# Attention and mixture of experts on one core: interleaved masked tiles, a product with ones for the last sort, and a leaner start

## The reference

```python
# layer 1: causal attention with rotary positions, then a layernorm
Q, K, V = x @ wq.T, x @ wk.T, x @ wv.T        # 16 heads of 8
Q, K = apply_rope(Q), apply_rope(K)
scores = where(causal, Q @ K.T / sqrt(8), -inf)
x = layernorm(x + softmax(scores) @ V @ wo.T)
# layer 2: plain attention over the layernormed rows, no mask
y = x + msa(layernorm(x, ln1_w, ln1_b), w_qkv, w_proj)
# experts: the row's best expert by argmax of the gate
z = layernorm(y, ln2_w, ln2_b)
e = argmax(z @ gate_w + gate_b)               # first one wins a tie
y = y + gelu(z @ w1[e]) @ w2[e]               # 128 -> 512 -> 128
out = layernorm(x + y)
```

## Time and profile before

| | |
|---|---|
| median of 3 runs | 896.61 us (893.73 to 900.15) |
| profiled execution | 894.7 us, span 893.0 us |
| PE, PEld | 809.2 us (91%), 369.5 us (41%) |
| ACT | 775.7 us (87%) |
| DVE | 328.5 us (37%) |
| POOL | 228.5 us (26%) |
| chain that ended last | PE 76%, DVE 8%, ACT 4%, issue 4%, DMA 2% |
| DMA | 51.60 MB, mean 58 GB/s |

### The profile page before, as it was taken

One profiled execution on the slowest core, in us unless ns is written; L12 is line 12 of the kernel. 1 busy time (PEld: TensorE's weight loads), 2 busy tenths in 40 slices (PEclk: granted clock), 3 DMA queues, 4 the chain that ended last, 5 costly groups with the idle time before them and its releaser, 6 DMA issues.

```text
span 893.0 us, 24266 instructions
## 1 busy us (share of the span) xinstructions
PE 809.2 (91%) x9940; PEld 369.5 (41%) x9952; DVE 328.5 (37%) x948; ACT 775.7 (87%) x906; POOL 228.5 (26%) x367
## 2 busy tenths in 40 slices
PE   8689999999999998999999999999999999996271
PEld 4244444444443443444344444444444444443240
DVE  5434525312430014320042433255332363334763
ACT  3579889999999998999999999999999899994440
POOL 5542211111110010000003343323334141443382
PEclk9799999999999999999999999999999999998575
DMA  8977220202110431810201000301000010001001
GB/s 273 269 210 224 96 49 2 95 2 49 49 48 1 108 84 40 244 50 3 48 2 32 1 3 3 78 8 37 3 3 19 14 43 3 1 3 31 30 14 41
DMA packets 34644, 51.60 MB, mean 58 GB/s; under 512 B 4064, under 2 KB 15072, under 8 KB 34528
## 3 DMA queue, kind: packets, MB, share of 16 engines
q1 hardware_dynamic: 32992, 46.30, 18.2%
q0 software_dynamic: 1536, 3.67, 1.3%
HBM read 29.12 MB, written 20.84 MB: 56 GB/s over the span
## 4 chain that ended last, share of the span: by engine, by line
PE 76%; DVE 8%; ACT 4%; issue 4%; DMA 2%; SPq 2%; POOL 2%; POOLq 1%; another core or an unknown queue 1%; DVEq 0%; ACTq 0%
PE ps L488 72%; ACT probs L922 3%; PE ps L493 3%; PE ps L787 1%; POOLq L1070 1%; DMA query_rows<-q_scratch 1%; POOL parts L1077 1%; DVE ln_newton L1156 1%; DMA q_scratch<-parts 1%; DVE q_rotated L1312 1%; DVE ln_newton L1155 1%; DVE z_rows L1176 1%; DVE ln_stats L1161 0%; DVE ln_newton L1154 0%
## 5 line engine op out<-in xcount | busy, mean ns | idle before, releaser
L922 ACT ACTIVATE probs<-ps 128x1024 f32<-128x1024 f32 (+3 forms) x832 | 736.0, 1017 | 41.5 <-PE ps L488 35.1
L488 PE MATMUL ps<-probs,values 128*9 128x256 f32 (+1 forms) x6528 | 426.3, 374 | 4.7 <-DVE q_rotated L1312 3.1
L488 PE MATMUL ps<-query_rows,key_rows 32*128 32x512 f32 (+3 forms) x1664 | 282.5, 485 | 17.5 <-ACT probs L922 10.2
L488 PEld LDWEIGHTS ps<-probs,values 128*9 128x9 f32 x6528 | 143.3, 90 | 182.5 <-issue 94.4
L488 PEld LDWEIGHTS ps<-query_rows,key_rows 32*128 32x128 f32 x1664 | 117.3, 183 | 183.5 <-issue 93.1
L1043 POOL TENSOR_SCALAR_AFFINE_SELECT probs<-probs 128x256 f32<-128x256 f32 x128 | 53.0, 420 | 234.4 <-ACT probs L922 231.5
L1090 POOL COPY parts<-early_late 128x512 f32 x63 | 44.5, 744 | 124.6 <-PE ps L488 124.6
L1048 POOL DMA_INDIRECT z_sorted<-z_rows,slot_numbers x16 | 15.8, 988 | 218.3 <-DVE slot_numbers L1447 208.8
L1312 DVE COPY q_rotated<-ps 128x512 f32<-128x512 f32 x30 | 20.7, 690 | 124.7 <-PE ps L488 124.6
L1077 POOL COPY parts<-parts 128x512 f32 x72 | 44.9, 663 | 29.3 <-PE ps L488 28.8
L1324 DVE RECIPROCAL recip<-ps 128x16 f32<-128x16 f32 x32 | 8.2, 256 | 70.5 <-PE ps L493 65.1
(11 more groups left out here) (184 smaller groups left out, 586.4 us busy)
## 6 DMA issues: line engine op xcount, KB each, us to landing
k_scratch<-parts SPq DMA_DIRECT2D x16, 512.0 KB, 3.9
q_scratch<-parts SPq DMA_DIRECT2D x16, 512.0 KB, 5.5
query_rows<-q_scratch SPq DMA_DIRECT2D x32, 256.0 KB, 5.3
key_rows<-k_scratch SPq DMA_DIRECT2D x20, 256.0 KB, 4.6
key_rows<-k_scratch SPq DMA_DIRECT2D x16, 192.0 KB, 4.5
parts<-in_w SPq DMA_DIRECT2D x1, 2048.0 KB, 8.9
early_late<-in_w SPq DMA_DIRECT2D x8, 256.0 KB, 8.0
early_late<-z_sorted SPq DMA_DIRECT2D x4, 384.0 KB, 3.1
```

Source lines behind the costliest of these rows:

```text
L488: return nc.tensor.matmul(out, l, r, start=start, stop=stop, skip_group_check=True)
L922: nc.scalar.activation(Pr[:, t % KEPT, 2 * p:2 * p + 2, lo:BLK], score_banks(t, p)[:, :, lo:BLK], ACT.Exp, bias=-SHIFT[r["a"]], scale=SCAL ...
```

## The change

1. **Order of tiles.** `ORDER` lists the key tiles of a causal run: a block's own four tiles stand between older, full ones, the narrow ones first. `run_step`, `cut` and the start and stop flags follow it.
2. **Start.** The small loads go to ACT's queue; DVE's copy of `blk` comes after the first rotations; `first_rows` loads head group 0 of block 0 first, on semaphores of its own.
3. **One key copy in memory.** `keys_out` writes once, `key_rows_in` doubles on reading by a source with a repeat of 2 outermost. This holds for all blocks of both attentions.
4. **1/sqrt.** The start is followed by one cubic turn (four linked steps) and one Newton turn; in `rows_to_h` the events before it are those due at one step before z (12 for the last block, 13 for the others, as before).
5. **Arg-max** by reduce and compare over all four row tiles at once, with a mask for ties; the running sums take fewer links.
6. **Last block's sort** by a product: DVE compares each row's slot with 0..767 (`spread`), PE multiplies z with it over four row tiles into two banks. No scatter, no load. The second last block's `finish` comes after the two sorted results are taken. The numbers 0..767 are loaded after the last attention.
7. **Gathers** of y for blocks 0 and 1 are paced at steps 4, 6, 8, 10 and not at 1, 2, 3, 4.

```diff
+ORDER = (
+    (0, 1, 2, 3),
+    (0, 1, 2, 3, 6, 4, 7, 5),
+    (0, 1, 2, 3, 4, 5, 11, 6, 10, 7, 9, 8),
+    (0, 1, 2, 3, 4, 5, 6, 7, 8, 15, 9, 14, 10, 13, 11, 12),
+)
-        k_scratch = nc.dram_tensor("k_scratch", (2, NP, NP, DK, H, S), F32, kind="Internal").ap()
+        k_scratch = nc.dram_tensor("k_scratch", (2, NP, DK, H, S), F32, kind="Internal").ap()
...
+        spread = [KAv[:, 1 + i // 2, i % 2 * SORTED:(i % 2 + 1) * SORTED] for i in range(TB)]
...
-                for i in range(NP):
-                    sp.dma_start(k_scratch[a - 1, i, :, :, :, b * BLK:(b + 1) * BLK].rearrange("j d h t -> (d h) j t"),
-                                 k3[:, b]).then_inc(k_out[b], 16)
+                sp.dma_start(k_scratch[a - 1, :, :, :, b * BLK:(b + 1) * BLK].rearrange("j d h t -> (d h) j t"),
+                             k3[:, b]).then_inc(k_out[b], 16)
...
+            def key_rows_in(a, g0, g1, t0, t1, done):
+                src = k_scratch[a - 1].rearrange("j d (g f) t -> f (j d) g t", f=HG)
+                for f in range(HG):
+                    sp.dma_start(kaf[f * ROWS:(f + 1) * ROWS, g0:g1, t0:t1],
+                                 src[f, :, g0:g1, t0:t1].unsqueeze(0).to_broadcast([NP, NP * DK, g1 - g0, t1 - t0])).then_inc(done, 16)
...
+            def first_rows():
+                sp.wait_ge(k_out[0], 16)
+                key_rows_in(1, 0, 1, 0, BLK, k_first)
+                sp.wait_ge(q_out[0], 32)
+                query_rows_in(1, 0, 0, 1, q_first)
+                for g in range(1, G):
+                    key_rows_in(1, g, g + 1, 0, BLK, k_rows[0])
+                query_rows_in(1, 0, 1, G, q_rows[0])
...
+            def m_spread_sums(b, k, n):
+                if n:
+                    return
+                for i in range(TB):
+                    pe.wait_ge(m_spread, i + 1)
+                    for m, c in ((0, slice(0, BLK)), (1, slice(BLK, SORTED))):
+                        last = mm(ps[:, side_bank(b, m), 0:c.stop - c.start], zb[:, i, :], spread[i].bitcast(F32)[:, c],
+                                  i == 0, i == TB - 1)
+                        if i == TB - 1:
+                            last.then_inc(m_side, 1)
...
-                        pace(first_step(2, b + 2) + 1 + i)
+                        pace(first_step(2, b + 2) + 4 + 2 * i)
...
+            def cubic(y, c, t, u):
+                link(tt(t, y, y, ALU.mult))
+                link(tt(t, t, c, ALU.mult))
+                link(nc.vector.scalar_tensor_tensor(out=u, in0=t, scalar=-1.25 / CUBIC, in1=t, op0=ALU.add, op1=ALU.mult))
+                link(nc.vector.scalar_tensor_tensor(out=y, in0=u, scalar=1.875, in1=y, op0=ALU.add, op1=ALU.mult))
...
-                due(13)
+                cubic(y, c, t, u)
+                due(PREP_AT[b][0] - 1)
...
+                link(nc.vector.tensor_reduce(mx, lg[:, :, :], AX.X, ALU.max))
+                link(tt(oh[:, :, :], lg[:, :, :], mx.unsqueeze(2).to_broadcast([P, TB, E]), ALU.is_equal))
+                link(tt(lg[:, :, :], oh[:, :, :], first_wins[:, :].unsqueeze(1).to_broadcast([P, TB, E]), ALU.mult))
+                link(nc.vector.tensor_reduce(mx, lg[:, :, :], AX.X, ALU.max))
+                link(tt(oh[:, :, :], lg[:, :, :], mx.unsqueeze(2).to_broadcast([P, TB, E]), ALU.is_equal))
...
+                if b == NB - 1:
+                    dve.wait_ge(ld_n, 16)
+                    for i in range(TB):
+                        ts(spread[i], places, destf[:, i:i + 1], None, ALU.is_equal).then_inc(m_spread, 1)
...
             route(b)
+            experts(b, AT_END[:2], at_once)
             add_experts(b - 1)
             finish(b - 1)
-            experts(b, AT_END, at_once)
+            experts(b, AT_END, at_once, 2)
```

More of the change, by code:

```diff
@@ L38 @@
 THETA = 10000.0
+CUBIC = float(np.sqrt(3.0 / 8.0))
 P = 128
@@ L349, in run_step @@
         def run_step(r, n):
-            causal, kt = r["a"] == 1, r["k0"] + n
+            causal = r["a"] == 1
+            order = ORDER[r["qb"]] if causal else range(r["k0"], r["k1"])
+            kt = order[n]
             cut = causal and kt >= r["qb"] * TB
-            done = sum(TB for q in RUNS[:r["n"]] if q["a"] == 1)
+            done = r["n"] * TB + sum(k >= r["qb"] * TB for k in order[:n])
             return dict(r=r, t=r["t0"] + n, kt=kt, lo=(kt % TB) * P if cut else 0,
-                        cut=2 * (done + kt % TB) + 1 if cut else None, start=n == 0, stop=kt == r["k1"] - 1)
+                        cut=2 * done + 1 if cut else None, start=n == 0, stop=n == len(order) - 1)
         block = ctx.enter_context(nc.Block())
@@ L1059, in experts @@
                     pool.wait_ge(z_clear, 16 * ROUNDS // 2)
-                row_out(b, 0)
-                if b == NB - 1:
-                    for i in range(1, TB):
-                        row_out(b, i)
+                if b < NB - 1:
+                    row_out(b, 0)
                 pool.wait_ge(m_owner, b + 1)
@@ L1118, in _ @@
                 for r in runs_in(1, qb):
-                    for i in range(TB):
-                        cut(run_step(r, qb * TB + i))
+                    for n, kt in enumerate(ORDER[qb]):
+                        if kt >= qb * TB:
+                            cut(run_step(r, n))
                     if r["n"] == 0:
@@ L1169, in normalize @@
                 link(ins)
-                v, y, h, t = (nw[:, n, :] for n in range(4))
+                v, y, h, t, c, u = (nw[:, n, :] for n in range(6))
                 link(ts(v, mv[:, :, 1], EPS, None, ALU.add))
-                rsqrt(y, v, h, t, 1)
+                root_start(y, h, c, mv[:, :, 1], v)
+                cubic(y, c, t, u)
                 between()
-                newton(y, h, t, 2)
+                newton(y, h, t, 1)
                 for i in range(TB):
@@ L1345, in rows_to_h @@
                 due(11)
-                y, v, h, t = (nw[:, n, :] for n in (1, 4, 5, 6))
-                link(tt(v, y, y, ALU.mult))
-                link(tt(v, v, mv[:, :, 1], ALU.mult))
-                link(ts(v, v, EPS, None, ALU.add))
-                rsqrt(y, v, h, t, 2)
-                due(13)
+                y, var, v, h, c, t, u = (nw[:, n, :] for n in (1, 6, 0, 2, 4, 3, 5))
+                link(tt(var, y, y, ALU.mult))
+                link(tt(var, var, mv[:, :, 1], ALU.mult))
+                link(ts(v, var, EPS, None, ALU.add))
+                root_start(y, h, c, var, v)
+                cubic(y, c, t, u)
+                due(PREP_AT[b][0] - 1)
                 newton(y, h, t, 1)
@@ L1467, in gelu, with experts @@
                                                ).then_inc(m_hid, 1)
-            def experts(b, order, due):
-                for k, (at, name, r) in enumerate(order):
+            def experts(b, order, due, k0=0):
+                for k, (at, name, r) in list(enumerate(order))[k0:]:
                     if name == "turn" and b < NB - 1:
@@ L1573, in _ @@
             dve.wait_ge(ld_e, 16 * 10)
+            ts(first_wins[:, :], iota[:, :], -1.0, float(E), ALU.mult, ALU.add)
             dve.wait_ge(init, 3)
@@ L1635 @@
             (p[:, None] // ROWS == np.arange(HG)[None, :]).astype(np.float32)], axis=1),
+        places=np.concatenate([np.tile(np.arange(SORTED), (P, 1)), p[:, None] + P * np.arange(ROUNDS)[None, :]],
+                              axis=1).astype(np.float32),
     )
```

117 lines of the change are left out of this document (63 added, 54 removed).

## The result

The changed kernel is slower: median 978.9 us (976.29 to 980.05, 4 runs) against 895.17 (891.32 to 900.15), ratio 1.0928 with a 95% interval of 1.0867 to 1.0989. The profiled execution has a span of 976.0 us for 893.0. The forecast was 869.

The account below looks back on a forecast made before the run. ACT was taken to bound full tiles, PE the causal blocks, DMA the head, and a chain of short steps the tail. Terms -7 - 13 - 4 - 3 = -27 gave 867.7, stated as 869 us; range 856 to 886, holding 0.8.

Parts of the forecast that it names:

- The second rival: Key rows read by the repeat of 2 use two DMA engines: slower, 973 us, say 940 to 990; chance 0.12.
- The head: Start up to the first runs: fewer bytes and earlier loads bring first scores near 28.5; -7 us, ends 0 and -9.
- The second part: Head: DVE's wait for x_rows, ending at 77.8, moves with the 2.1 MB less ahead of it, 7 us, to near 70.
- Masked tiles: Three later causal blocks: narrow tiles beside full ones remove waits of ACT; -13 us, ends -4 and -17.
- The first rival: Narrow tiles stay PE-bound, the order only moves the bubbles: masks give -4, 878 us; chance 0.13.
- Root, routing, gathers: Shorter root, less waiting on z in the second attention, gathers of y moved: -4 us, ends 0 and -6.
- their -1.5: Gathers of y moved to steps 4 to 10 remove DVE's late copy of 2.16 us and a like delay next block.
- The tail: After the last attention: shorter root and arg-max, sort by product, finish moved behind the sorted rows; -3 us.
- the +3 end: Tail's slow end: half clock throughout and both POOL blockings, +3 us; the other end is -6.

Follow-up runs that it names:

- two copies: The changed kernel with keys stored twice again and key rows read with 32 rows outermost, all else kept: 890.05 us, 0.997 of the kernel before.
- the grouping: The changed kernel with two key copies, and head groups 1 to 3 of block 0's keys in one DMA a head: 886.39 us, 0.9885.
- 4 x 8 rows: The kernel before, its two key copies in memory with a gap behind every eight rows of a head's source: 932.83 us, 1.0409.

## Why the prediction was wrong

**The key rows.** The forecast costed the one key copy by bytes: fewer stored, the same read, at the 267 GB/s of the earlier trace rows. The failed step is that one: it took every transfer for one on sixteen engines. The second rival said what happens otherwise and had 0.12; it gave 973 us, and 978.9 came. Its mechanism held, but that its sum is so near is luck: three errors cancel. It had x_rows 85 us late, and it was 59 (at 136.75, not 163), since an engine moves 24.5 GB/s and not 18 and a set of 1.05 MB takes 21 us and not 29. It had 10 us for the late keys of the second attention, where 28 came. And it kept 17 us of gains, where 3 were there. It also lacked the two stops in the first block (9 and 10 us, for its other head groups and for the second block's query rows), which cost nothing on top, since DVE still waits 46.19 us for x_rows behind them. I held against it that the trace had no such source. That was no argument: a shape of transfer that a trace lacks is an unknown with a wide price, and the repeat was the one shape in the change that no row covered.

**The head** (forecast -7). First scores near 28.5: 29.08 in the changed kernel. That part was right. The second run was to begin at 36.5 and begins at 39.84 with two copies: the first run takes 9.4 us, where I allowed 8 and it takes 8.97 before. No drop of the clock was to follow, but it fell all the same, as this window of the kernel with two copies shows (granted clock 0.50):

```profile
32.00:40.00 8.00, 6.62 (x59) 2.77 (x61) 2.49 (x7) 4.61 (x10) 4.08 (x9) 0.50 1.00 331
```

The second part failed: that the wait for x_rows would move to 70 with the bytes. It moved to 79.97. Part of that stream is bound by SP's issue, which I had costed only up to the first run; the grouping gives 3.6 us of the 10 back. Nor was it one stream of bytes: in the kernel before SP already waits 24.4 us in all, ahead of its four sets of key rows, for the key stores to land, and the DMA share from 50 to 55 us is 0.45. How much of the other 6 us such waits make was not tried. Of -7 there remained +3.8 by the third run of the second block.

**Masked tiles** (forecast -13). The first rival, narrow tiles stay PE-bound, -4, is what came in size, and in part by its reason: at the narrowest tile half of what is left is PE's values and half the score slots. The forecast and it shared one error. I read 21.5 us above ACT's floor and kept only 8.5 for what an unmasked block shows. The right subtraction was at hand: the wait at a run's end is 0.76 us in the earlier trace rows, and it is replaced by 0.42 at the narrowest tile's new place. I put each narrow tile "where PE has 1.81 us of ACT's time to hide in"; but the values in its way are those of the full tile two positions back, 1.05 us, and ACT has 0.53. Blocks 1, 2 and 3 were to take 53, 81 and 109 us and take 56.3, 83.9 and 111.5.

**Root, routing, gathers** (forecast -4). Right in sum: with two copies the first run of the second attention takes 30.54 us for 32.78 (-2.2; the wait on z of the earlier trace rows is gone), the first runs of its other blocks take 30.79, 30.49 and 30.51. With the next sentences that makes -3.6. For their -1.5 the gathers get no credit: DVE's late copy of the earlier trace rows (2.16 us) waits 1.36 in the kernel with the order alone, where the gathers are as before, and the third and fourth block's first runs take 30.92 and 30.91 there for 31.62 and 32.49; with the product alone they take 30.93 and 30.92. So that wait was an accident of one profile. Against those the change gives 0.4 to 0.6 a block, by the shorter root or the gathers; which was not tried.

**The tail** (forecast -3). The owners are set 21.7 us after the last exp with two copies, as forecast (836.3 less 814.6), 22.9 in the changed kernel. The steps of the changed kernel, to be laid beside the earlier trace rows:

```profile
899.03 1.11 PE L524 MATMUL ps<-ident,attn_rows 128*128 128x128 f32 x4 [0.99 <-DVEq L1379]
...
918.36 2.21 DVE L1525 TENSOR_SCALAR key_rows<-probs,row_low 128x768 fp32r<-128x768 f32 x4
919.04 7.33 PE L519 MATMUL ps<-key_rows,z_rows 128*128 128x512 f32 x16 [3.86 <-DVE key_rows L1525]
...
925.98 0.81 DVE L1559 TENSOR_SCALAR h_cols<-ps,ln_wb 128x512 f32<-128x512 f32 x1 [5.41 <-PE ps L519]
...
930.77 0.53 DVE L1217 TENSOR_TENSOR ln_newton<-ln_newton 128x4 f32<-128x4 f32 x1
931.33 0.16 DVE L1218 TENSOR_TENSOR ln_newton<-ln_newton 128x4 f32<-128x4 f32 x1
...
935.16 0.68 DVE L1532 SCALAR_TENSOR_TENSOR squares_blockdiag<-squares_blockdiag,early_late 128x512 f32<-128x512 f32 x1
```

The first row takes 1.11 us where the same four products took 0.66 before: the granted clock is 0.50 from 899 to 902 us already, and with the projection behind it that is the 1.3 us by which all later steps are late. The product takes 7.33 us (forecast 7.1) and a comparison 0.55 (0.8, between 0.4 and 1.1). The row with 0.53 is one of six steps of `finish` that POOL's copies stretch, from 0.16 to between 0.46 and 0.61: `finish` with its sum takes 7.8 us and not the 6 I gave it. So the step that failed is POOL's share in it: 1 us allowed, 2.7 measured (2.2 in these six, the rest in the last scaling). The Trainium skill, SBUF — State Buffer, section Who interferes with whom, has a DVE step with two SBUF inputs and a GpSimd copy exclude each other; the stretched step at 930.77 has two and agrees. Two of the six, at 929.45 and 930.09, read one tensor only, so more than that is at work. The tail of the changed kernel is 2.2 us longer than before, near the +3 end, but 1.3 of that is the clock; with two copies it is 1.2 shorter, where -3 was forecast.

## What to carry to other kernels

Before a transfer is costed by bytes, read its source's outermost dimension, after merging, and compare it with 16; then the issue time of all DMAs up to the gate, not only up to the first use. Price an idle gap by the steps of a run without other work and ask what stands in order ahead of the engine that ends it; a total above a floor is not a gain to be had. When work moves beside something long, put all that fits there: the place of `finish` was worth more than the product.

## What the runs showed of the hardware

- The outermost dimension of a DMA's source counts its engines, with real steps as with a repeat: 2 gave a share of 0.13 and 49 to 51 GB/s, 4 gave 0.27 and 88 to 97, some 22 to 25 GB/s an engine.
- Such a DMA also holds its queue: four of 256 KB took SP 10.13 us, with 4 x 8 rows 2.9, with 32 rows outermost 2.5. The four query loads behind the first of these took it 7.94 us, behind the last 2.46.
- Value products that write to different groups of 32 partitions of PSUM run abreast: 4 of 128 columns take 0.61 us and 16 take 0.62.
- Taking products off PE, so that it idles within runs that ACT bounds, brought the granted clock of blocks 2 and 3 from 1.00 to 0.75 and 0.79 and made them 5 and 7 us longer (88.97 for 83.92, 118.84 for 111.52).
